# Loads of x in a pass over groups of nodes: issued by ScalarE into its own queue instead of GpSimd's

## The reference

```python
# graph part
xn  = rmsnorm(layernorm(x)) * rms_w
h   = xn @ W_down                      # 10000 x 256
xl, xr = h @ Wl, h @ Wr                # 4 heads of 64
e   = leaky_relu(xl[src] + xr[dst]) . att
out = segment_softmax_sum(e, xl[src], dst)   # edges and a loop for each node
x1  = x + out @ W_up                   # 10000 x 1024
# expert part
xn2 = layernorm(x1)
top2 = top_k(xn2 @ expert_tokens.T, 2) # of 8 experts
out = x1 + sum over the two experts of mlp(xn2) / 2   # 1024 -> 64 -> 64 -> 1024, gelu
```

## Time and profile before

| | |
|---|---|
| median of 3 runs | 1637.22 us |
| lowest, highest | 1632.99, 1646.51 us |
| the profiled execution | 1640.42 us |
| its span, first to last instruction | 1638.7 us |
| mean granted TensorE clock | 0.961 |
| PE, DVE, ACT, POOL busy | 1489.0, 1193.0, 687.0, 681.2 us |
| moved by DMA | 306.94 MB, mean 187 GB/s |

### The profile page before, as it was taken

One profiled execution on the slowest core, in us unless ns is written; L12 is line 12 of the kernel. 1 busy time (PEld: TensorE's weight loads), 2 busy tenths in 40 slices (PEclk: granted clock), 3 DMA queues, 4 the chain that ended last, 5 costly groups with the idle time before them and its releaser, 6 DMA issues.

```text
span 1638.7 us, 28903 instructions
## 1 busy us (share of the span) xinstructions
PE 1489.0 (91%) x9321; PEld 1235.5 (75%) x9321; DVE 1193.0 (73%) x2415; ACT 687.0 (42%) x1365; POOL 681.2 (42%) x769
## 2 busy tenths in 40 slices
PE   6999999999699656998989957999999999999997
PEld 5999999999577335877767746777777777777775
DVE  5666666666388675898988974777777777777775
ACT  2444445454243630000000005666566566656653
POOL 2112222223675004677666543444444444444432
PEclk9999999999799887999999978999999999999999
DMA  8888875552564098799999757677677666765420
GB/s 204 227 179 193 174 199 152 163 140 67 133 207 119 1 266 201 208 293 287 264 255 286 211 151 220 211 220 224 213 217 217 208 206 207 218 207 157 120 56 15
DMA packets 121961, 306.94 MB, mean 187 GB/s; under 512 B 64155, under 2 KB 65857, under 8 KB 114315
## 3 DMA queue, kind: packets, MB, share of 16 engines
q1 hardware_dynamic: 60088, 155.40, 34.2%
q0 software_dynamic: 61728, 149.74, 32.6%
HBM read 220.40 MB, written 138.85 MB: 219 GB/s over the span
## 4 chain that ended last, share of the span: by engine, by line
PE 46%; issue 20%; DMA 11%; POOL 9%; DVE 8%; SPq 1%; POOLq 0%; DVEq 0%; ACT 0%
PE psum L1888 14%; DMA agg<-node_table,from_idx 8%; PE psum L1856 7%; PE psum L1564 7%; PE psum L1565 6%; PE psum L1566 6%; PE psum L1886 4%; DVE stat L967 2%; POOL where_from L606 2%; POOL agg L663 2%; DVE cx L1325 2%; POOL xls L639 1%; POOL td L643 1%; POOL rstd L595 1%; PE psum L1744 1%
## 5 line engine op out<-in xcount | busy, mean ns | idle before, releaser
L1888 PE MATMUL psum<-w_raw,gl 128*128 128x512 f32 x528 | 269.2, 591 | 0.0
L911 ACT ACTIVATE xt_hi<-psum 128x512 fp32r<-128x512 f32 x264 | 151.0, 597 | 238.4 <-PE psum L1856 238.3
L1492 DVE TENSOR_TENSOR xt_lo<-psum,xt_hi 128x512 fp32r<-128x512 f32 x264 | 176.3, 688 | 86.3 <-ACT xt_hi L911 86.2
L1603 PE MATMUL psum<-wdx_hi,axt_hi 128*125 128x272 f32 x640 | 191.4, 299 | 6.8 <-DVE wd_lo L1034 4.0
L1505 DVE SCALAR_TENSOR_TENSOR xb<-psum,xb 128x512 f32<-128x512 f32 x264 | 176.0, 686 | 28.0 <-PE psum L1888 27.7
L995 DVE TENSOR_TENSOR axt_lo<-psum,axt_hi 128x500 fp32r<-128x500 f32 x160 | 108.4, 678 | 118.8 <-ACT axt_hi L771 118.8
L1856 PEld LDWEIGHTS psum<-ident,xn 128*128 128x128 f32 x1056 | 126.4, 142 | 86.8 <-issue 68.3
L1605 PE MATMUL psum<-wdx_hi,axt_lo 128*125 128x272 f32 x640 | 185.5, 290 | 0.0
L1604 PE MATMUL psum<-wd_lo,axt_hi 128*125 128x256 f32 x640 | 180.2, 281 | 0.0
L743 POOL DMA_INDIRECT out<-xb,idx_in x132 | 133.8, 1014 | 106.1 <-issue 59.4
L905 ACT ACTIVATE xn<-xb 128x1024 f32<-128x1024 f32 x132 | 156.1, 1233 | 45.1 <-DMA xb<-rows_x,idx_in 45.1
(11 more groups left out here) (277 smaller groups left out, 3872.1 us busy)
## 6 DMA issues: line engine op xcount, KB each, us to landing
w_raw<-in_L_ffn_W SPq DMA_DIRECT2D x140, 256.0 KB, 12.7
cx<-in_x POOLq DMA_DIRECT2D x20, 1792.0 KB, 15.3
rows_x<-cx SPq DMA_DIRECT2D x19, 1806.0 KB
ax<-in_x SPq DMA_DIRECT2D x19, 1792.0 KB
node_table<-trow SPq DMA_DIRECT2D x19, 896.0 KB
node_table<-xld SPq DMA_DIRECT2D x10, 448.0 KB
cx<-in_x POOLq DMA_DIRECT2D x20, 208.0 KB, 23.1
rows_x<-cx SPq DMA_DIRECT2D x19, 209.6 KB
```

The lines of the kernel that those rows point to most:

```text
L1492: dve.tensor_tensor(xt_lo[:, 2 * q:2 * q + 2, :].rearrange("p k n -> p (k n)"), T_R[q % 2], xt_hi[:, 2 * q:2 * q + 2, :].rearrange("p k n ...
L1603: pe.matmul(into, high, wdx_hi[:, k, :], start=k == 0, stop=False, skip_group_check=True)
L1888: pe.matmul(Y[u], gl2[:, t % 2, rows], w3_raw[:, t % N3, HALF * n:HALF * (n + 1)], start=False, stop=True, skip_group_check=True).then_inc ...
```

## The change

`load_cx` moves word for word from GpSimd's program to ScalarE's; the gathers, the scatters and the stores stay in theirs. ScalarE issues loads 0 and 1 between its sixth and seventh batch in stage B, load 2 after its last, loads 3 to 5 once the gather of group 0 has landed (the new wait for `agg_loaded[0]`), and load g + 4 in the loop of stage C behind `split_agg(g + 1)` and behind the wait for the stores of group g - 2.

```diff
--- before.py
+++ after.py
@@ gpsimd @@
-            def load_cx(g):
-
-                for rows in (slice(0, SPLIT), slice(SPLIT, P)):
-                    pool.dma_start(cx[g % NCX][rows, :, 0:D],
-                                   x_g[g, rows, :].rearrange("p (j d) -> p j d", j=J)).then_inc(cx_loaded[g % NCX], 16)
...
-            pool.wait_ge(b_lsb, 2)
-            load_cx(0)
-            load_cx(1)
-            pool.wait_ge(b_sb, NB)
-            load_cx(2)
             pool.wait_ge(map_loaded, 16)
             pool.wait_ge(rows_stored, 32 * NB)
             gather_rows(0)
-            load_cx(3)
             gather_rows(1)
-            load_cx(4)
-            load_cx(5)
             for g in range(NG):
...
                 if g >= 1:
                     enlist(g - 1)
-                if 2 <= g and g + NCX - 2 < NG:
-                    pool.wait_ge(x1_put[(g - 2) % 3], 32 * ((g - 2) // 3 + 1))
-                    load_cx(g + NCX - 2)
@@ scalar @@
-            with act.Fori(0, NB) as b:
+            def weigh_own(b):
...
+            def load_cx(g):
+
+                for rows in (slice(0, SPLIT), slice(SPLIT, P)):
+                    act.dma_start(cx[g % NCX][rows, :, 0:D],
+                                  x_g[g, rows, :].rearrange("p (j d) -> p j d", j=J)).then_inc(cx_loaded[g % NCX], 16)
+
+            with act.Fori(0, 6) as b:
+                weigh_own(b)
+            act.wait_ge(b_lsb, 2)
+            load_cx(0)
+            load_cx(1)
+            with act.Fori(6, NB) as b:
+                weigh_own(b)
+            act.wait_ge(b_sb, NB)
+            load_cx(2)
+            act.wait_ge(rows_stored, 32 * NB)
+            act.wait_ge(agg_loaded[0], 16 * J)
+            for g in range(3, NCX):
+                load_cx(g)
...
             for g in range(NG):
                 if g + 1 < NG:
                     split_agg(g + 1)
+                if 2 <= g and g + NCX - 2 < NG:
+                    act.wait_ge(x1_put[(g - 2) % 3], 32 * ((g - 2) // 3 + 1))
+                    load_cx(g + NCX - 2)
```

## The result

The changed kernel takes 1628.28 us (median of 20 runs, 1624.52 to 1635.9) against 1639.98 us (20 runs of the kernel before, 1631.67 to 1650.49). The ratio is 0.9927, with a 95% interval of 0.9910 to 0.9945: 12 us or 0.7% faster, where 35 us were forecast. The forecast of 1602 us is wrong in size, and 1628 lies in the wide range, but well outside the 1597 to 1609 of the case that was called likeliest. One of the 12 executions of E9, further down, took 8400 us for a reason that no trace shows; the median of the other 11 is 1626.93 us.

The account below looks back on a forecast made before the run. Stage C was taken to be bound by gathers waiting behind loads: 1640.42 - 37.2 (gathers) + 1.1 (issues) + 1 (carry) = 1605.3 us profiled, which lies 3.2 above the median, so 1602; wide range 1596 to 1637.

Parts of the forecast that it names:

- the case that was called likeliest: Forecast A: in stage C the gathers leave the path, gaining 37.2 us; 1597 to 1609 us, chance 0.58.
- the gather's wait behind the load: Stage C: gathers queue behind a 2 MB load in the software queue, making groups 16.98 us, not 14.65; excess 37.2 us.
- L: Stage C: landing time of a group's last gather, 18.3 us before, forecast 10.8; period (15.7 + L) / 2 where over 14.65.
- the engines can carry it: Stage C: the DMA engines move a group's 4.62 MB in 13.5 us, under 14.65, or later loads stay hidden.
- Rival B: Stage C: bytes bind, the DMA rate stays at 276 GB/s; 1615 to 1626 us, chance 0.18.
- nothing on GpSimd: Stage C: two issues of 664 ns a group leave GpSimd's stream where it idles anyway; no gain.
- nothing from ScalarE's wait in the loop: Stage C: ScalarE's new wait for the store of g - 2 costs nothing unless a store needs over 32 us.
- the two without take 14.65 each, which is what the engines themselves need: Stage C: two groups without loads showed 14.65 us a group, taken as the pace reachable once gathers stop binding.
- The split of the 37.2 us: Stage C: the excess was 32.6 us of TensorE waits for gathers plus 4.6 us put down to the granted clock.
- the one-off costs at the turn from B to C: Start of stage C: six ScalarE issues for loads 3 to 5, +1.1 us (0 to +5.3), and the carry transfer, +1.
- Carry: Turn from B to C: a 3.49 us transfer on the chain, slowed by loads starting quicker; +1 us, bounds 0 to +3.5.
- C: Rival: in stage C gathers still land after about 18 us because three full queues hold the engines; 1637 us, chance 0.12.

Follow-up runs that it names:

- E9: The changed kernel timed once more, on another chip against the kernel before: 1627.47 us, ratio 0.9914.
- E6: The kernel before, with the loads of groups 6 to 19 cut to an eighth of the bytes, queues unchanged: 1620.55 us, ratio 0.9884.
- E7: The changed kernel with its first copy before loads 3-5, loads 0-1 after carry, and loads of groups 6-19 cut to an eighth: 1616.96 us, ratio 0.9854.
- E8: The changed kernel with its first copy before loads 3-5, loads 0-1 after carry, and loads of groups 6-19 in SyncE's queue: 1619.76 us, ratio 0.9855.
- E4: The changed kernel with its first copy before loads 3-5, loads 0-1 after carry, and one more VectorE comparison per group: 1626.04 us, ratio 0.9907.
- E12: The changed kernel with its first copy before loads 3-5, and loads 0-1 left in GpSimd's queue: 1618.55 us, ratio 0.9860.

## Why the prediction failed, step by step

**Right: the gather's wait behind the load was the limit, and the change takes it away.** The median of all gathers is 9.0 us, where 8 to 12 was forecast, and TensorE's waits for them fall to 5.6 us, where under 5 was. E6 shows the cause from another side: a smaller load in the same queue gives the time of a moved load with the one-off costs mended (1620.55 and 1619.75 us). L itself, the landing of the last gather of four, was put at 10.8 and came out at 12.6 in the mean, 15.0 at most. That (15.7 + 12.6) / 2 = 14.2 us still lies under the floor is thanks to the room that was left, and with 15.0 there is none.

**Right: the engines can carry it.** 293 to 319 GB/s at full share, and E7 shows that no time hangs on the bytes. Rival B is out. The Trainium skill's rule in DMA: Bandwidth & Descriptors, Rules for kernel authors, is that spreading transfers over engines doesn't help bandwidth. E8 agrees in this: the third queue adds nothing. But at the same full share the rate was 276 GB/s before and 304 from 696 to 880 us in the changed kernel and in E8 alike, with three queues or two. So a busy share of 1 was no limit of bytes here, and what counted was the order of the transfers.

**Right: nothing on GpSimd, and nothing from ScalarE's wait in the loop.** Ahead of its copies 1 to 19 ScalarE still waits for TensorE's transposes alone.

**Wrong, the step that failed most: "the two without take 14.65 each, which is what the engines themselves need".** Two distances between ScalarE's copies showed TensorE's pace while it had work ahead, not the stage's. VectorE's pace is 15.27, and it stood in the trace of before, in the chain through the last groups:

```profile
932.21 1.19 DVE stat L967 x2
...
947.47 1.19 DVE stat L967 x2
```

15.26 us for one group, in the stretch that was read as 14.65. The earlier trace rows had a hint too: VectorE was busy for 246.54 of the 271.60 us, 15.4 a group, which doesn't fit into 14.65. With 15.3 the term is 27, and 25.1 were measured, so 12 of the 20 us by which the forecast missed the span lie here. E4 shows it: VectorE had nothing to spare.

The split of the 37.2 us was read wrongly too. By the earlier trace rows TensorE stood idle for 271.60 - 244.57 = 27.0 us, and its 16 groups took 10.2 us more than 16 x 14.65 while it was busy, where the prediction put 4.6 down to the clock. In the changed kernel, from copy 1 to 17, it is idle for 5.2 of 246.49 us and busy for 241.28, still 6.9 more than 16 x 14.65: that part didn't go with the gathers' waits, as it had to if 14.65 was to be reached.

**Wrong in size: the one-off costs at the turn from B to C.** They were put at +2.1 with bounds of 0 to 8.8, and were +9.2, beyond both bounds together. The six issues were priced by SyncE's 0.36 us and took 0.93 each, dearer than GpSimd's 0.66 too: 4.5 on the path where 1.1 was taken, within the bound of 5.3. Carry was put at +1 and bounded by +3.5, for which no row was given, and lost 4.85. It was known to be on the chain and to have loads issued next to it; only that the loads were already there before made it look safe, and E12 shows that they harm it only from the hardware queue at the same moment.

The rest of the miss is small: -1.4 between copies 0 and 1, -0.6 ahead of carry, +0.5 at the end of stage C and +2.2 in stage D.

That 1628 us lies in the wide range is no merit of the case that was called likeliest: it lies between the times of rivals B (1615 to 1626) and C (1637), which the range took in and whose mechanisms didn't happen.

## What to carry to other kernels

In this kernel a transfer that a loop waits for was better off in a queue without the bulk transfers that have time, and which other queue these went to mattered little. After removing a wait, take the next floor from each engine's own chain, as the distance between one instruction and its like a group later on the busiest engine, and compare busy time per group on every engine with the pace that is assumed. And when transfers move to an engine with little to do, look at the one moment at which it is on the path: a handful of issues ahead of its first result cost more than all of those in the loop.

## What the runs showed of the hardware that wasn't expected

- One issue of a 112-partition load on ScalarE held its stream for 0.62 to 0.70 us, the 13-partition one behind it for 0.85 to 1.74, 5.6 us for six; all 40 of the changed kernel took 0.61 to 2.16 us, median 0.78, against 0.36 for SyncE's stores and 0.66 for GpSimd's loads.
- A transfer of 41 KB into one partition took 7.9 to 8.3 us beside loads that ScalarE issued within 0.01 us of it, 3.4 alone, and 3.5 beside the same loads from GpSimd's queue, issued 0.27 us later.
- Where TensorE ran 4% quicker than VectorE, it didn't just wait. In three of 16 groups the granted clock went to 0.50, the lower of its two levels, after a stop of about 0.3 us, and such a group took 16.8 us in place of 14.6. Stops of up to 1.7 us elsewhere left the clock at 1.00. The mean of all groups still came out at VectorE's pace.
- At the same full share of the DMA engines the rate was 276 GB/s with the loads in the software queue and 304 with them in a hardware queue.
